# Local attention of a two-layer network: the queries' norm as factor of the row maxima, the order of a pair's steps on GpSimd, and the place of the values' projection

## The reference

```
qkv = h @ wqkv;  q, k, v = split(qkv)          # h: the tokens, half of the channels shifted by one
q = q / |q| * q_scale;   k = k / |k| * k_scale # norms over the 64 channels of a head
q = q * cos * s + rotate_half(q) * sin * s     # rotary tables
k = k * cos / s + rotate_half(k) * sin / s
sim  = 8 * q @ k.T                             # own window and the one before it, masked
attn = softmax(sim);   o = attn @ v;   x = x + o @ wo
```

## Time and profile before

| | |
|---|---|
| median of 3 runs | 1557.06 us (1556.17 and 1557.06, and one of 2086.83) |
| profiled execution | 1554.51 us, its span 1552.7 us |
| TensorE busy | 1470.4 us, 95% of the span |
| VectorE, ScalarE, GpSimd busy | 66%, 58%, 34% |
| the attention of the two layers | about 890 to 1105 us and 1228 to 1440 us of the span |

### The profile page before, as it was taken

How to read it: one execution, slowest core, us unless ns; L and a number is a source line. 1 busy time by engine, 2 the same in 40 slices (tenths; PEclk the granted TensorE clock), 3 DMA queues, 4 the chain that set the end, 5 groups by cost and what they waited for, 6 DMA issues and landing times. The chain is left out here.

```text
span 1552.7 us, 24403 instructions
## 1 busy us (share of the span) xinstructions
PE 1470.4 (95%) x9004; PEld 963.3 (62%) x9004; DVE 1018.0 (66%) x1855; ACT 903.2 (58%) x1888; POOL 522.4 (34%) x323
## 2 busy tenths in 40 slices
PE   8889999999998899999999889999999889999998
PEld 3432222222225679798888567777777678777776
DVE  3768888888835446556564656666687556666675
ACT  5137777777784443425353378888543478978341
POOL 7100000000003410000004277988252478887222
PEclk9899999999999999999999999999999999999999
DMA  7720222110000403030304110000200100000010
GB/s 246 164 41 1 42 41 42 22 22 2 1 12 14 126 21 104 14 109 14 109 0 147 56 57 1 2 1 1 83 1 0 58 1 2 1 1 28 14 42 27
DMA packets 59476, 64.84 MB, mean 42 GB/s; under 512 B 15154, under 2 KB 48706, under 8 KB 59380
## 3 DMA queue, kind: packets, MB, share of 16 engines
q1 hardware_dynamic: 58020, 60.17, 14.8%
q10 hardware_dynamic: 1360, 3.41, 0.6%
HBM read 52.88 MB, written 10.49 MB: 41 GB/s over the span
## 5 line engine op out<-in xcount | busy, mean ns | idle before, releaser
L581 DVE TENSOR_REDUCE mcol<-bank 128x1 f32<-128x1024 f32 x256 | 302.1, 1218 | 57.9 <-PE bank L572 57.9
L669 ACT ACTIVATE a_pt<-bank 128x512 f32<-128x512 f32 x512 | 266.4, 602 | 89.2 <-PE bank L701 89.2
L701 PE MATMUL bank<-qa,ka 99*128 99x512 bf16 x512 | 193.7, 386 | 7.6 <-ACT a_pt L669 3.8
L572 PE MATMUL bank<-ka,qa 96*128 96x512 bf16 x512 | 193.2, 385 | 5.2 <-DMA ka<-k_parts 1.7
L2045 DVE CUSTOM_DVE_ANT_0 w_sm<-bank,mask 128x256 f32<-128x256 f32 (+1 forms) x256 | 88.8, 403 | 110.5 <-PE bank L1628 110.5
L1587 PE MATMUL bank<-wqkv,w_hst 128*128 128x512 f32 x576 | 153.8, 412 | 2.7 <-DVE w_sinp L1985 2.3
L701 PEld LDWEIGHTS bank<-qa,ka 99*128 99x128 bf16 x512 | 49.1, 98 | 165.7 <-ACT a_pt L669 121.3
L712 PE MATMUL bank<-a_pt,vst 128*32 128x512 f32 x1024 | 136.4, 605 | 0.1
L1879 ACT ACTIVATE w_sm<-w_sm,w_st 128x256 f32<-128x256 f32 (+1 forms) x256 | 123.9, 488 | 17.8 <-DVE w_st L2045 17.6
L1587 PEld LDWEIGHTS bank<-wqkv,w_hst 128*128 128x128 f32 x576 | 106.9, 193 | 26.7 <-issue 5.1
L1485 POOL TENSOR_TENSOR w_sm<-w_sm,w_st 128x1024 f32<-128x1024 f32 (+1 forms) x64 | 115.4, 1803 | 19.0 <-DVE w_st L2052 18.9
(11 more groups left out here) (254 smaller groups left out, 2868.1 us busy)
## 6 DMA issues: line engine op xcount, KB each, us to landing
f_wex<-in_W SPq DMA_DIRECT2D x8, 2048.0 KB, 12.2
qa<-q_parts SPq DMA_DIRECT2D x48, 128.0 KB, 4.3
ka<-k_parts SPq DMA_DIRECT2D x48, 128.0 KB, 4.8
q_parts<-p_parts SPq DMA_DIRECT2D x16, 192.0 KB, 3.3
k_parts<-p_parts SPq DMA_DIRECT2D x8, 384.0 KB, 3.4
wqkv_raw<-in_wqkv SPq DMA_DIRECT2D x2, 1536.0 KB, 6.8
w_raw<-in_w SPq DMA_DIRECT2D x2, 1408.0 KB, 6.0
phi<-in_phi SPq DMA_DIRECT2D x5, 512.0 KB, 3.7
```

Of the source, the lines that this page charges most:

```text
L572: last = nc.tensor.matmul(max_bank(G, r)[:, jh * HALF:(jh + 1) * HALF], G["qa"][k][0:KS, hg % 2, h, it * P:(it + 1) * P], G["ka"][k][0:KS, ...
L581: nc.vector.reduce_max(G["mcol"][hg % 2][:, p:p + 1], max_bank(G, r)[:, :], X).then_inc(G["max_free"], 1)
L669: nc.scalar.activation(pt[n % 2][:, q, :], sbank(HG * step + q), ACT.Exp, scale=HD0 ** -0.5).then_inc(p_ready, 1)
L701: mm(sbank(i), ka[k][:, q, n * P:(n + 1) * P], qa[k][:, ih, q, :], start=True, stop=True).then_inc(st_ps, 1)
```

## The change

Four things change.

1. `normalised(i)` on GpSimd multiplies only the keys (the second half of a tile's row, 128x512) by the inverse norms. The queries' inverse norm becomes the factor of `maxima`: in place of the constant `-QK_SCALE` the custom instruction reads `rn` of the head, one value for each partition. The constant moves into the queries' tables and the mask changes its sign. VectorE waits for `rn_done` ahead of the maxima.
2. In every odd slot `normalised(t-1)` stands ahead of `turn(t)` (before, only in slot 1; in the others behind it).
3. `rows_of` on TensorE waits for `add_done` ahead of the queries' transposes and for `turn_done` only ahead of the keys'.
4. `values(t)` on TensorE moves behind `prob_rows(t-3, 2 and 3)` and `scores(t-2, 1)`; on ScalarE its copy moves behind the exponentials of heads 4 to 7.

```diff
@@ -1504,8 +1504,8 @@
                     def normalised(i):
                         pool.wait_ge(add_done, before(i) + 1)
                         pool.wait_ge(rn_done, NG // 2 * l + i // 2 + 1)
-                        rows = turned[:, i % 3, :].rearrange("p (h d) -> p h d", d=HD1)
-                        V.tensor_tensor(rows, rows, rn[:, i // 2 % 2, i % 2, :].unsqueeze(2).to_broadcast([P, 2 * H1, HD1]),
+                        rows = turned[:, i % 3, INNER:2 * INNER].rearrange("p (h d) -> p h d", d=HD1)
+                        V.tensor_tensor(rows, rows, rn[:, i // 2 % 2, i % 2, H1:2 * H1].unsqueeze(2).to_broadcast([P, H1, HD1]),
                                         ALU.mult).then_inc(turn_done, 1)
 
                     pool.wait_ge(G["tables_in"], 4 * (l + 1))
@@ -1518,11 +1518,9 @@
                             norm_low(UNITS * l)
                         if there(t):
                             cosines(t)
-                            if t == 1:
+                            if t % 2:
                                 normalised(t - 1)
                             turn(t)
-                        if there(t) and t % 2 and t > 1:
-                            normalised(t - 1)
                         if there(t - 2):
                             probabilities(t - 2, 0)
                         if there(t) and t % 2:
@@ -1607,8 +1605,9 @@
                     project(l, V_PS, i, 2).then_inc(v_ps, 1)
 
                 def rows_of(l, i):
-                    pe.wait_ge(turn_done, (NG * l + i) + 1)
-                    for j, (ready, free) in enumerate(((tq_ps, pt_dve), (tk_ps, pt_act))):
+
+                    for j, (rows, ready, free) in enumerate(((add_done, tq_ps, pt_dve), (turn_done, tk_ps, pt_act))):
+                        pe.wait_ge(rows, (NG * l + i) + 1)
                         pe.wait_ge(free, 2 * (NG * l + max(i - 1, 0)))
                         for p in range(HP):
                             last = tr(T_PS[j][:, p * P:(p + 1) * P],
@@ -1690,17 +1689,17 @@
                             hidden(UNITS * l, 0, 1)
                         if there(t - 4):
                             mixed(t - 4)
+                        if there(t - 3):
+                            prob_rows(t - 3, 2)
+                            prob_rows(t - 3, 3)
+                        if there(t - 2):
+                            scores(l, t - 2, 1)
                         if t == NG - 3:
                             pe.wait_ge(xc_done, KD * (UNITS * l + 1))
                         if t == NG - 1:
                             pe.wait_ge(sd_done, UNITS * l + 1)
                         if there(t):
                             values(l, t)
-                        if there(t - 3):
-                            prob_rows(t - 3, 2)
-                            prob_rows(t - 3, 3)
-                        if there(t - 2):
-                            scores(l, t - 2, 1)
                         if t == NG + 2:
                             pe.wait_ge(hn_low, KD * (UNITS * l + 1))
                             pe.wait_ge(w_round, NPIECES * (l + 1))
@@ -1903,12 +1902,12 @@
                             scaled(UNITS * l)
                         if there(t) and t % 2:
                             norms(l, t // 2)
-                        if there(t):
-                            values(l, t)
                         if there(t - 3):
                             prob_rows(t - 3, 3)
                         if there(t - 2):
                             exponentials(t - 2, range(4, 8))
+                        if there(t):
+                            values(l, t)
                         if 5 <= t < 5 + NPIECES:
                             copy_piece(l, t - 5)
                         if 7 <= t < 7 + NPIECES:
@@ -2040,10 +2039,11 @@
                     def maxima(i, half):
                         s = i % 2
                         dve.wait_ge(s_ps, 2 * before(i) + half + 1)
+                        dve.wait_ge(rn_done, NG // 2 * l + i // 2 + 1)
                         for h in range(4 * half, 4 * half + 4):
                             c0 = (h % 4 // 2) * 2 * WIN
                             V.tensor_tensor_reduce(sm[:, s, h, keys(i)], S_PS[h % 2][:, c0:c0 + 2 * WIN][:, keys(i)],
-                                                   mask_of(i), -QK_SCALE, HIGHEST, ALU.add, ALU.min,
+                                                   mask_of(i), rn[:, i // 2 % 2, s, h:h + 1], HIGHEST, ALU.add, ALU.min,
                                                    st[:, s, 1, h:h + 1]).then_inc(s_masked, 1)
 
                     def inverse_sums(i, j):
@@ -2269,9 +2269,9 @@
     scale = np.concatenate([scale, scale], -1)
     cos, sin = np.cos(freqs), np.sin(freqs)
     sin = np.concatenate([-sin[:, :HD1 // 2], sin[:, HD1 // 2:]], -1)
-    c["tables"] = np.stack([cos * scale, sin * scale, cos / scale, sin / scale]).astype(f)
+    c["tables"] = np.stack([-QK_SCALE * cos * scale, -QK_SCALE * sin * scale, cos / scale, sin / scale]).astype(f)
     i, j = np.arange(WIN)[:, None], np.arange(WIN)[None, :]
-    last, own = np.where(j >= i, 0.0, MASKED), np.where(j <= i, 0.0, MASKED)
+    last, own = np.where(j >= i, 0.0, -MASKED), np.where(j <= i, 0.0, -MASKED)
     c["mask"] = np.concatenate([last, own, last], 1).astype(f)
     c["ident"] = np.eye(P, dtype=f)
     one = np.repeat(np.eye(CE, dtype=f), NP_, 1).reshape(CE, CS // P, P)
```

## The result

| | before | changed |
|---|---|---|
| median | 1556.62 us (6 runs) | 1542.36 us (6 runs, 1539.85 to 1544.86) |
| ratio to before | | 0.9917, 95% interval 0.9898 to 0.9936 |
| profiled execution, its span | 1554.51 us, 1552.7 us | 1542.83 us, 1541.0 us |

The ratio is that of the mean times, 1542.36 and 1555.26 us, with the kernel before's one run of 2086.83 us left out.

A forecast was written before the change was run, and what follows sets the result against it. TensorE, busy 95% of the span, was taken as the bound. Gross 26.6 us less returns of 1.1, 1.2, 2.0 and 3.1 gave 19.2 off 1554.5, so 1535.3; the median stands 2.6 higher: 1538, range 1528 to 1550.

The forecast's parts named there:

- The wait on the norm, 21.3 us: TensorE's row transposes in both attention layers: all waits for GpSimd's norm go, 11.5 + 9.8 us gained.
- The clock in slot 4, 5.3 us: Slot 4's TensorE groups: without the wait the clock stays up, gaining 2.6 and 2.7 us in the two layers.
- The first rival: Slot 4's clock falls anyway, after slot 3 waits about 1.4 us for the bank: 5.3 us back, 1543; chance 0.17.
- The factor per partition: VectorE's maxima reading a per-partition factor: 0.07 us more each, inside the bank's cover of 0.45, zero on the path.
- The second rival: Maxima over 0.10 us dearer make `prob_rows(.., 2)` wait for the bank in each full slot: 7.3 us back, 1545; chance 0.13.
- The last rival, the port: VectorE's maxima wait for GpSimd's instructions at the shared SBUF port: 40 us on top, 1578; chance 0.03.
- The change of shape, 3.1 us: TensorE's values followed by 64-column weighted sums: 0.12 us in 26 slots lost, bounds nothing and 0.2 us (5.2).
- Slot 3, 1.1 us: Slot 3, where ScalarE waited for VectorE and now copies the values later: 0.57 us a layer lost.
- Slot 12, 1.2 us: TensorE wants the keys at about 1025.3, `w_kT` ends at 1025.74: about 0.6 us a layer lost.
- one of the prediction's own signs: Transposes of probabilities on TensorE: no wait of L1650 outside slot 3.
- The tail, 2.0 us: Slots 14, 16 and the tail, bound by ScalarE and GpSimd anyway: about 1 us a layer lost.
- The change of less than 2%: Whole kernel: the change stays within about 2% (31 us), called what a measurement can tell from none; chance 0.94.

The follow-up runs named there:

- The two partial versions: On the kernel before: only the full norm ahead of the turn, 1543.59 us; only half norms and split waits, 1541.33 us.
- Part 4 alone: Only the move of the values' projection and copy behind the second scores, on the kernel before; 1558.46 us, ratio 1.0036.
- the run without part 4: Changed kernel with the values' projection and copy back in their old places; 1534.87 us, ratio 0.9885; again 1535.90 us, 0.9893.
- values between: Changed kernel with TensorE's values group between the transposes of probabilities and the second scores; 1539.15 us, ratio 0.9911.
- constant factor: Changed kernel with the constant 1.0 as factor of the maxima instead of the queries' inverse norms; 1540.60 us, ratio 0.9916.
- the last version: Kernel without part 4, with a shared square-root table and late values in slot 15; 1530.40 us, ratio 0.9851; again 1531.78 us, 0.9863.

## Why the prediction was right or wrong

*The wait on the norm, 21.3 us.* Right, and by the mechanism named: the even tile was held up by its neighbour's turn. The waits are gone in both layers, and either edit alone frees the ordinary slots. (Slot 2's 1.72 us became 0.73, which is counted below.)

*The clock in slot 4, 5.3 us.* Right in the changed kernel: 1.09 and 3.04 us for the two groups, in both layers and both profiles. The two partial versions show what it hung on: with 1.11 or 1.68 us of wait left the clock fell in the first layer and held in the second. The first rival's worry, slot 3's wait for the bank (1.4 us feared, 1.64 measured), came true without its consequence.

*The factor per partition.* Right: 0.06 us against 0.07, inside the cover in the full slots (in slot 6 the copy behind the maxima ends at 946.79, and TensorE wants the bank at 947.08). The second rival, the bank taking the norm's place in each full slot, did not happen; only slot 3 waits for it, as the first rival had said. The last rival, the port, had no trace: the slowest of 256 maxima took 486 ns beside GpSimd's work.

*The change of shape, 3.1 us.* The term was real and its size off: 0.21 us a slot instead of 0.12, 5.5 us in all, beyond the upper bound of 5.2. The pair that it priced, the values' group in front of the weighted sums, costs 0.13 us more, as estimated. The other 0.08 us is the output projection, which has transposes behind it in place of the values and took 1.79 us for 1.71. I had looked at one pair of neighbours where a whole slot's order had to be compared.

*Slot 3, 1.1 us.* This step failed. It counted ScalarE's later copy alone. In the first layer the waits of slots 2 and 3, without the norm's, were 0.61, 0.56 and 0.85 us and are now 0.73, 1.28, 0.79 and 1.64: 2.4 us more; in the second 1.44, 0.54 and 0.85 became 1.41, 1.15 and 1.64: 1.4 more. 3.8 us in place of 1.1. The wait for the bank was seen, but only as a rival's cause for the clock, and left out of the sum; the wait for the maxima in slot 2 was not seen at all. Both come of the same thing: a group that covered a wait was taken from a slot that has no output projection to cover it. Part 4 alone has both waits as well, and the run without part 4 has neither at that length.

*Slot 12, 1.2 us.* About right in kind, short in size: 0.26 us of issue, 0.66 us for GpSimd's probabilities and 0.20 us for the values' copy in slot 13, in each layer, 2.2 us. Of the three only a wait like the first had been foreseen, and its two times, 1025.3 and 1025.74, are 0.44 us apart where 0.6 was taken. The wait for GpSimd's probabilities also breaks one of the prediction's own signs, no wait at the transposes of probabilities outside slot 3. Nor does the return belong to part 4, under which it was listed: without part 4 slot 12 still loses 0.50 and 0.55 us to other waits.

*The tail, 2.0 us.* Too small. TensorE's lead over the kernel before is 7.4 us at the start of slot 16 and 5.1 at the output projection of slot 18: 2.3 us lost, and 2.2 in the second layer, 4.5 together. The wait behind ScalarE was foreseen, the clock was not: in each layer 1.6 to 1.7 us are two groups at 1.2 GHz. The step looked at the clock where it fell before and not where a new wait could make it fall. This return isn't part 4's either, since the wait is 2.32 us without it.

Together 5.5 + 3.8 + 2.2 + 4.5 = 16.0 us are given back instead of 7.4, and 26.6 - 16.0 = 10.6 us remain of the gross sum. The profiled executions differ by 11.7 us. The rest lies outside the change: 0.7 us were lost before the attention begins and 1.6 us won in the feed-forward, where a group of 24 matmuls behind an equal wait took longer in the kernel before (the first line) than in the changed one (the second):

```profile
1215.88 7.39 PE L1748 MATMUL bank<-m_hid,w 128*128 128x512 f32 x24 [2.00 <-DVE w_sinp L1985]
...
1210.83 5.81 PE L1747 MATMUL bank<-m_hid,w 128*128 128x512 f32 x24 [2.00 <-DVE w_sinp L1984]
```

This is the clock again, and it is chance: the wait is 2.00 or 2.01 us in all twelve profiles of this case, and the group took 7.36 to 7.39 us in six of them and 5.81 to 5.83 in the other six. The changed kernel had the short form in both of its profiles, the run with the values back the long one in the first and the short one in the second. Why it falls in one execution and not in another stays open; it puts about 1.6 us of chance into any comparison of single profiles here.

So the forecast's mechanism for the gain held, and its returns were too small by 8.6 us. The median came nearer to 1538 than that by luck: 1.6 us are the feed-forward's clock, and the 2.6 us by which the median was put above the profiled execution did not come (1542.36 and 1542.83). The change of less than 2%, to which 0.94 were given, came true; but the 31 us named as what a measurement can tell from no change was far too much, since the interval here is 0.2% to either side.

## What to carry to other kernels

When a wait is taken off an engine that is nearly always busy, write the slot's new order out whole and compare it group by group with the old one: covers taken away in the first slots and dearer pairs of neighbours gave back 9.3 of the 16.0 us. A group that seems free to move may be the cover of another's wait where the loop is not yet full. A wait that is left can cost its own length again in clock, or nothing, from one layer or run to the next, so look for long waits at the end of a loop too, and don't read a difference of one or two us from single profiles before the granted clock of both has been compared.

## What was not expected of the hardware

Two neighbours in another order cost 0.21 us in a slot, although the same matmuls ran. The granted clock fell to 1.2 GHz behind some waits and held behind others of the same length. In slot 4 it fell in both layers behind 2.94 us (before) and 2.45 and 2.43 us (part 4 alone), and in the first layer only behind 1.68 and 1.11 us. In slot 12 it held in both layers behind 2.44 us (before); with part 4 alone it held behind 2.25 us in the first layer and fell behind 2.26 in the second. In slot 16 it fell in both layers behind 2.10 us (changed kernel, 2.08 when run again), 1.84 and 2.31 us, and in the first layer only behind 2.32, 2.27 and 2.08 us (values back, values between, constant factor). It held through 1.28 and 1.64 us in slots 2 and 3 of the changed kernel and through 0.77 and 0.78 in slots 15 and 16 of the last version. A custom VectorE instruction with a factor per partition took 0.48 us instead of 0.42, and its constant form 0.42 again.
